# A gated cross-attention and ternary feed-forward kernel: front and second turn as one list, and ternary weights in two passes

## What is computed

```python
x = x + tanh(g_xattn) * xattn(layernorm(x), ctx, mask)    # 16 heads of 32, 77 keys, softmax
x = x + tanh(g_ffn) * ffn(layernorm(x))

def weight_quant(w):                                       # per matrix, 512 x 2048
    scale = 1.0 / clip(mean(abs(w)), 1e-05)
    return clip(round(w * scale), -1.0, 1.0) / scale       # -1, 0 or 1
def act_quant(x):                                          # per token
    scale = 127.0 / clip(max(abs(x)), 1e-05)
    return clip(round(x * scale), -128.0, 127.0) / scale
def ffn(x):                                                # 512 -> 2048 -> 512
    gate = silu(act_quant(x) @ weight_quant(w_gate).T)
    up = act_quant(x) @ weight_quant(w_up).T
    return act_quant(gate * up) @ weight_quant(w_down).T
```

## Time and profile before

| | us |
|---|---|
| median of three runs | 1346.26 |
| lowest, highest | 1342.62, 1346.9 |
| the profiled execution | 1347.23 |
| its span, first to last instruction | 1345.4 |

### The profile page before, as it was taken

One profiled execution on the slowest core, in us unless ns is written; L12 is line 12 of the kernel. 1 busy time (PEld: TensorE's weight loads), 2 busy tenths in 40 slices (PEclk: granted clock), 3 DMA queues, 4 the chain that ended last, 5 costly groups with the idle time before them and its releaser, 6 DMA issues.

```text
span 1345.4 us, 26267 instructions
## 1 busy us (share of the span) xinstructions
PE 1253.8 (93%) x7552; PEld 620.8 (46%) x8126; DVE 1122.8 (83%) x2631; ACT 870.6 (65%) x1350; POOL 737.6 (55%) x1186
## 2 busy tenths in 40 slices
PE   4767699999999999999999999999999999999996
PEld 2223344445454454545454454545445454544542
DVE  6777597897979898897979899797979889796883
ACT  4886756658584766757575665757475665857562
POOL 2104654647475564657466564757566465747662
PEclk9867899999999999999999999999999999999998
DMA  9785348565665658564674756565574847565432
GB/s 327 234 253 114 72 80 172 115 151 115 130 138 111 146 117 169 114 147 113 122 158 89 172 117 150 116 143 124 109 155 109 179 106 152 113 133 98 87 83 67
DMA packets 386793, 181.64 MB, mean 135 GB/s; under 512 B 324323, under 2 KB 357987, under 8 KB 385123
## 3 DMA queue, kind: packets, MB, share of 16 engines
q1 hardware_dynamic: 386736, 181.04, 60.0%
HBM read 61.32 MB, written 35.46 MB: 72 GB/s over the span
## 4 chain that ended last, share of the span: by engine, by line
PE 52%; DVE 18%; DMA 12%; issue 6%; ACT 5%; SPq 4%; POOL 2%; POOLq 0%; ACTq 0%; DVEq 0%
PE bank L1247 16%; PE bank L1259 11%; PE bank L1107 6%; PE bank L1108 6%; PE bank L1109 6%; DMA aT<-ah 6%; PE bank L1186 4%; DVE nmax L987 4%; DVE region L1048 3%; DMA xT<-xh 2%; DVE ah L1011 2%; DVE hmx L1054 2%; POOL work L621 1%; DVE xn L972 1%; ACT work L744 1%
## 5 line engine op out<-in xcount | busy, mean ns | idle before, releaser
L630 POOL TENSOR_TENSOR region<-region,up 128x512 f32<-128x512 f32 x256 | 328.4, 1288 | 290.9 <-DVE region L1048 197.6
L1247 PE MATMUL bank<-tern_gate,region 128*128 128x512 fp8e4 x1024 | 264.6, 381 | 12.3 <-DMA region<-zb 9.3
L1247 PE MATMUL bank<-tern_up,region 128*128 128x512 fp8e4 x1024 | 263.7, 380 | 0.8 <-ACT up L783 0.8
L1259 PE MATMUL bank<-tern_down,region 128*128 128x512 fp8e4 x1024 | 234.5, 382 | 13.7 <-DMA region<-hb 9.6
L1048 DVE SCALAR_TENSOR_TENSOR region<-region,bank 128x512 f32<-128x512 f32 x256 | 170.5, 679 | 79.5 <-ACT region L775 79.2
L775 ACT ACTIVATE region<-bank,fs 128x512 f32<-128x512 f32 x256 | 176.5, 693 | 65.7 <-PE bank L1247 65.6
L621 POOL TENSOR_TENSOR work<-work 124x512 f16<-124x512 f32 x160 | 184.4, 1172 | 26.9 <-ACT work L744 19.9
L1054 DVE TENSOR_REDUCE hmx<-region 128x1 f32<-128x512 f32 x256 | 170.1, 675 | 27.0 <-POOL region L630 26.9
L783 ACT ACTIVATE up<-bank 128x512 f32<-128x512 f32 x256 | 153.9, 602 | 38.0 <-PE bank L1247 37.9
L788 ACT ACTIVATE hb<-region 128x2048 bf16<-128x2048 f32 x64 | 122.8, 1919 | 43.8 <-DVE region L1070 43.8
L1259 PEld LDWEIGHTS bank<-tern_down,region 128*128 128x128 bf16 x1024 | 97.8, 98 | 109.9 <-issue 3.5
(11 more groups left out here) (145 smaller groups left out, 2357.1 us busy)
## 6 DMA issues: line engine op xcount, KB each, us to landing
q_stack<-q_rows SPq DMA_DIRECT2D x96, 256.0 KB, 4.4
xbig<-in_x SPq DMA_DIRECT2D x16, 1024.0 KB, 5.3
q_rows<-q SPq DMA_DIRECT2D x64, 256.0 KB, 3.2
out_y<-o SPq DMA_DIRECT2D x64, 256.0 KB, 3.2
q_stack<-mT SPq DMA_DIRECT2D x32, 256.0 KB, 4.2
region<-in_wgT SPq DMA_DIRECT2D x4, 1024.0 KB, 9.5
region<-in_wuT SPq DMA_DIRECT2D x4, 1024.0 KB, 7.4
region<-in_wdT SPq DMA_DIRECT2D x4, 1024.0 KB, 6.0
```

Source lines behind the costliest of these rows:

```text
L630: nc.gpsimd.tensor_tensor(ht, ht, up[:, n % 2, :], ALU.mult).then_inc(hmul_ready, 1)
L1247: ins = T.matmul(pb[2 * (n % 2) + w][:, :], xqT[:, k, tok], tern[w][:, k * FF + n * GT:k * FF + (n + 1) * GT], start=(k == 0), stop=(k == ...
L1259: ins = T.matmul(pb[2][:, :], hT[:, t % 2, k, :], tern[2][:, k * GT:(k + 1) * GT], start=(k == 0), stop=(k == FK - 1))
```

## The change

1. On every engine the front's list and the second turn's are one list now. The front's parts get three more letters: B is A of group 1, C is N of group 2, K is Q of group 2, and F is the feed-forward part of group 0. `second()` goes. Within the list pieces stand in another order, the front's too.
2. Ternary weights: each quarter is scaled and rounded in one pass on VectorE (`wr`), and ScalarE takes the sign of what is left behind MAGIC, with the constant from a column of `con`. The bounds at -1 and 1, the rounding pass on ScalarE and the semaphores between them go.
3. `mh` has a semaphore of its own, since it stands at another place among VectorE's steps.

GpSimd's list starts as before: `wx`, `wm`, `kx`, the first norm of group 1, `wx`, `vx`, `wm`, `wm`, the subtractions.

```diff
 TENSOR_FIRST = """
-    A:pv00 A:pv01 A:sc13 A:sc14 A:pv02 A:pv03 Q:s30 A:pv10 A:pv11 A:pv12 A:pv13 Q:s31 A:wo00 A:wo10 A:wo20
-    A:wo30 Q:mT00
+    Q:s30 A:pv00 A:sc13 A:pv01 A:sc14 Q:s31 A:pv02 A:pv03 A:pv10 A:pv11 A:pv12 A:pv13 Q:mT00 A:wo00 A:wo10
+    A:wo20 A:wo30 B:sc00 B:sc01 B:sc02 F:gu00 F:gu01 B:sc03 B:sc04 F:gu02 B:sc10 F:gu03 B:sc11 B:pv00 B:pv01
...
 SCALAR_FIRST = """
-    W:wu21 A:ah03 A:ah10 W:wu23 A:ah11 A:ah12 W:wt20 A:ah13 W:wt21 W:wt22 W:wt23 A:zq00 Q:mT00 A:zb00 A:zq10
-    A:zb10 A:zq20 A:zb20 A:zq30 A:zb30
+    W:wt21 A:ah13 W:wt22 Q:mT00 W:wt23 A:zq00 A:zb00 B:sc00 B:sc01 B:sc02 A:zq10 F:up00 F:gu00 F:gu01 A:zb10
+    B:sc03 F:up01 B:sc04 F:gu02 F:gu03 B:sc10 F:up02 B:sc11 F:up03 B:ah00 A:zq20 B:sc12 F:gu10 B:ah01 A:zb20
...
-FRONT = "AMNRQW", {"A": 0, "M": 0, "R": 0, "N": 1, "Q": 1, "W": None}
+FRONT = "AMNRQWBCKF", {"A": 0, "M": 0, "R": 0, "N": 1, "Q": 1, "B": 1, "C": 2, "K": 2, "F": 0, "W": None}
...
-            def weight_round(_, i, j):
-
-                act.wait_ge(wmean_ready, i + 1)
-                nc.scalar.activation(region[:, j * FF:(j + 1) * FF], region[:, j * FF:(j + 1) * FF], ACT.Copy, bias=MAGIC,
-                                     saturate=False, scale=c(R_G + i)).then_inc(wround_ready, 1)
-
             def weight_ternary(_, i, j):
 
-                act.wait_ge(wclip_ready, 4 * i + j + 1)
-                nc.scalar.activation(tern[i][:, j * FF:(j + 1) * FF], region[:, j * FF:(j + 1) * FF], ACT.Copy, bias=-MAGIC,
+                act.wait_ge(wround_ready, 4 * i + j + 1)
+                nc.scalar.activation(tern[i][:, j * FF:(j + 1) * FF], region[:, j * FF:(j + 1) * FF], ACT.Sign, bias=c(MINUS_MAGIC),
                                      saturate=False).then_inc(tern_ready, 1)
...
-            def weight_upper(_, i, j):
+            def weight_round(_, i, j):
 
                 dve.wait_ge(wmean_ready, i + 1)
-                V.tensor_scalar(region[:, j * FF:(j + 1) * FF], region[:, j * FF:(j + 1) * FF], c(R_G + i), 1.0,
-                                ALU.mult, ALU.min).then_inc(wupper_ready, 1)
-
-            def weight_lower(_, i, j):
-
-                if j % 2:
-                    dve.wait_ge(wround_ready, 2 * i + j // 2 + 1)
-                    V.tensor_scalar(region[:, j * FF:(j + 1) * FF], region[:, j * FF:(j + 1) * FF], MAGIC - 1.0, MAGIC + 1.0,
-                                    ALU.max, ALU.min).then_inc(wclip_ready, 1)
-                    return
-                dve.wait_ge(wupper_ready, 2 * i + j // 2 + 1)
-                V.tensor_scalar(region[:, j * FF:(j + 1) * FF], region[:, j * FF:(j + 1) * FF], -1.0, MAGIC,
-                                ALU.max, ALU.add).then_inc(wclip_ready, 1)
+                V.tensor_scalar(region[:, j * FF:(j + 1) * FF], region[:, j * FF:(j + 1) * FF], c(R_G + i), MAGIC,
+                                ALU.mult, ALU.add).then_inc(wround_ready, 1)
...
             turn(TENSOR_FIRST, *FRONT)
-            turn(TENSOR_ORDER, *second())
```

More of the change, by code:

```diff
@@ L531, in _ @@
             pieces["M"], pieces["R"] = pieces["N"], pieces["Q"]
+            pieces["B"], pieces["C"], pieces["K"] = pieces["A"], pieces["N"], pieces["Q"]
             pieces["E"] = pieces["G"] = pieces["H"] = pieces["I"] = pieces["F"]
@@ L539, in _ @@
             turn(SYNC_FIRST, *FRONT)
-            turn(SYNC_ORDER, *second())
             for g in range(2, NG - 1):
@@ L634, in _ @@
             pieces["M"], pieces["R"] = pieces["N"], pieces.get("Q")
+            pieces["B"], pieces["C"], pieces["K"] = pieces["A"], pieces["N"], pieces.get("Q")
             pieces["E"] = pieces["G"] = pieces["H"] = pieces["I"] = pieces["F"]
@@ L643, in _ @@
             turn(POOL_FIRST, *FRONT)
-            turn(POOL_ORDER, *second())
             with pool.Fori(2, NG - 1) as g:
@@ L802, in _ @@
             turn(SCALAR_FIRST, *FRONT)
-            turn(SCALAR_ORDER, *second())
             with act.Fori(2, NG - 1) as g:
@@ L1095, in _ @@
             turn(VECTOR_FIRST, *FRONT)
-            turn(VECTOR_ORDER, *second())
             for g in range(2, NG - 1):
```

87 lines of the change are left out of this document (55 added, 32 removed).

## The result

The changed kernel takes 1348.71 us (median of 20 runs, 1345.49 to 1351.39), the kernel before 1345.00 (median of 20, 1342.62 to 1346.90). The ratio is 1.0028, with a 95% interval of 1.0022 to 1.0035. So the change makes the kernel 3.7 us slower, where 7.5 us of gain were forecast; 1338.8 us and the range up to 1345.0 are both missed. The profiled execution of the changed kernel has a span of 1347.5 us, that of before 1345.4, with nearly equal mean clocks (0.977 and 0.974).

What follows compares the result with a forecast made beforehand. TensorE was taken as the bound from 167.3 us on, so gains lay ahead: cumulatively 0.3, 1.7, 2.6, 5.1, then 7.5 us along the front's chain. 1346.26 - 7.5 = 1338.8 us, range 1331.5 to 1345.

Steps and rivals of the forecast that it cites:

- Part 1: Ternary passes: 12 us off ScalarE, 6.6 off VectorE, little of it on the chain; Sign taken as 1.90 us.
- Part 2: Front up to GpSimd's first subtraction: projection 8 us earlier, sums later; subtraction at 99.4 against 99.74, gain 0.3 us.
- a landing near 76: Group 1's last transpose of x lands near 76, so its query projection starts 8 us earlier than 83.84.
- Rival C: Slower: group 1's projection isn't earlier, its transposes queued behind key transfers and W_up's first quarter; 1350.3 us, chance 0.10.
- 15.7 us from the projection's start to the last sum's end: Group 1's query projection to W_down's last sum on ScalarE: 76 to 91.7, where it was 8.3 us.
- The gap at GpSimd: GpSimd's 6.85 us wait between last reduction and first subtraction taken as fixed after the reduction, whatever the exponentials do.
- Rival A: Front gains too: GpSimd's gap runs beside the exponentials' wait, or projection starts some 4 us earlier; 1334.5 us, chance 0.18.
- Part 3: First subtraction to output projection: subtractions end at 111.3, output projection starts at 119.5; 2.6 us gained in all.
- Part 4: Output projection to first gate matmul: 18.2 us instead of 20.7, gate at 137.7; 5.1 us gained in all.
- Part 5: Second turn's attention: seven score matmuls fill TensorE's gap, first tile's integers done at 161.7 against 170.1; total 7.5 us.
- Rival B: ScalarE's order in the second turn eats the filling, leaving about 3 us of gain; 1343.3 us, chance 0.16.
- From here TensorE's own work sets the end as before, so the gain stays: Behind the first down projection: the whole 7.5 us gain is kept to the kernel's end.

Runs made afterwards that it cites:

- weights_only: Kernel before with only the new ternary passes, all lists in the old order; 1344.69 us, ratio 0.9997.
- scale_behind_q: Changed kernel with one VectorE piece, the scale of W_o, moved behind the low parts of the first two query columns; 1346.05 us, ratio 1.0013.
- one_sum_ahead_x: Changed kernel with W_o's scale later, W_down's last quarter ahead of query rows, two W_down sums earlier, x's load behind the second norm's transpose; 1340.35 us, ratio 0.9964.
- signs_ahead: scale_behind_q with W_up's ternary passes, the W_down loads and three of four W_down sums brought forward; 1351.32 us, ratio 1.0043.
- last_sum_first: signs_ahead with ScalarE's last W_down sum moved directly behind the projection's first output and the transposed maxima; 1349.23 us, ratio 1.0040.
- x_behind_z: Changed kernel with the 1 MB load of group 2's x moved behind the first transpose of z on the queue; 1345.14 us, ratio 0.9999.

## Why the prediction was wrong, point by point

The kernel came out 11.2 us above the forecast (7.5 of gain forecast, 3.7 of loss measured). In the profiles 5.5 us of these are there at the first down projection (172.87, forecast 174.9 - 7.5 = 167.4), and 4.1 us come behind it. The other 1.6 us are the draw: the profiled execution of before, from which the walk was made, was 2.2 us slower than its median, that of the changed kernel 0.6.

- **What bounds the kernel.** Right: from 167 us on TensorE is busy 1011 of 1033 us in the changed kernel as well. But it was 1015 before: nothing could shorten that stretch, and the change made 4.0 us more of idle time in it. All that the experiments moved lies ahead of it.
- **Part 1, ternary weights.** The sizes were right: the Sign passes took 1.99 us (the upper bound, I took 1.90), VectorE's 1.28 (1.31), and there is one table load. That the part gives next to nothing on the chain was wrong in the old order: weights_only's last reduction is 5.1 to 6.4 us earlier. It is no gain of time, though: the ratio is 0.9997 (0.9985 to 1.0010).

```profile
L717 ACT ACTIVATE tern_up<-region,con 128x2048 fp8e4<-128x2048 f32 x4 | 8.0, 1994 | 1.0 <-DVE region L953 1.0
...
L726 ACT ACT_TABLE_LOAD x1 | 1.3, 1283 | 0.7 <-PEq L1328 0.7
```

- **Part 2, the first failed step: "a landing near 76".** It was 79.4. The walk went through the tiles and the transposes and has no term for `wp10`, the 0.15 us operation that waits 6.0 us on VectorE for GpSimd. With it moved the start is 75.5. Rival C (15.7 us fixed behind the projection, each us lost is a us on the end) was the right frame with too low a chance, but the reason that it gave, transposes behind key transfers, isn't what the runs showed.
- **Part 2, the second: "15.7 us from the projection's start to the last sum's end".** 96.5 - 79.4 = 17.1 in the changed kernel and 19.9 in scale_behind_q. I had summed ScalarE's own work and taken the quarters as there. In the changed kernel the last one can be asked for from 82.3 on, when the last ternary pass of W_up is written, goes out behind query rows at 83.23, and takes 11.35 us to land. With it ahead of the rows the distance was 15.9.
- **The gap at GpSimd.** Right: 6.86 us between reduction and subtraction, put to "issue", and the exponentials had been done. Rival A's first half (that the gap runs beside the wait for the exponentials) is out. "Whatever comes" was too simple, see below.
- **Part 3.** 123.86 - 104.14 = 19.7 us from the first subtraction to the output projection, forecast 119.5 - 99.4 = 20.1, before 22.4. 2.6 us were won where 2.3 were forecast, on top of a start that was 4.7 us late.
- **Part 4, the third failed step: "the transpose takes 5.0 us as before".** It took 7.39. 21.4 us from output projection to gate, forecast 18.2. I counted the two DMAs that were moved out of the way and not the megabyte of x that was moved in ahead of the transpose; with it behind, the transpose took 3.17. Most of the other 0.8 us is a later issue, 13.9 us behind the output projection's start where 13.2 were forecast. The lower clock at the gate came nearly as forecast: four gate matmuls in 1.89 us, the next four in 1.61, then 1.03.
- **Part 5.** Better than forecast. Seven score matmuls are done in the gap; the first tile's integers start at 165.57, 20.3 us behind the gate, where it was 25.4 and 22.1 was forecast. The down projection comes 27.6 us behind the gate (32.1 before). Rival B, ScalarE's order eating the filling, didn't come true. But there are other new waits, 1.07 us at 166.23 for VectorE and 1.84 at 195.51 for a transpose, and from 167 to 245 us, where the prediction said to look, TensorE is idle 4.7 us where it was 1.6.

```profile
165.57 1.95 ACT L798 ACTIVATE hb<-region 128x2048 bf16<-128x2048 f32 x1
```

- **The fourth failed step: "From here TensorE's own work sets the end as before, so the gain stays".** 4.1 us are lost behind the first down projection: 2.0 us earlier than before there, 2.1 us later at the end. The cause is open in part, see the next section.

From the changed kernel to one_sum_ahead_x the medians go 1348.7 - 2.7 (scale) - 1.1 (quarter) - 0.5 (sums) - 4.0 (x) = 1340.4. These terms add up by themselves, since each is the step from one median to the next. What tests them is the load of x alone: 3.6 us from the changed kernel, and 1344.4 - 3.6 = 1340.8 was expected before the run, 1340.35 measured. Against before (1345.0 in 20 runs; the forecast started from 1346.26) that is a gain of 4.8 us by the ratio, of the 7.5 forecast.

## What stays open

The down projection of the changed kernel is 2.0 us earlier than before, and its end 2.1 us later. By the last residual of turn 2 some 2.6 us are lost; the largest single wait there is the 1.84 us at 195.51, before group 2's projection. The rest is lost in the loop, in turns in which keys and values of another batch are fetched: 0.9 us in turn 4 and 1.6 in turn 12, but none in turn 8. Measured at the last residual of each turn, the distance to the profile of before grows by 1.1 to 2.8 us from turn 1 to turn 15 in all 15 profiles of kernels with the new ternary passes, weights_only among them, whose loop has the same lists; in a second profile of the kernel before it grows by 0.1. The queue shows one place, in turn 4 (the second profile of before, then weights_only):

```profile
358.07 1.25 SPq L516 DMA_TRANSPOSE region<-zb  x1
360.25 1.29 SPq L453 DMA_DIRECT2D q_stack<-q_rows  x3
```

```profile
355.96 1.25 SPq L515 DMA_TRANSPOSE region<-zb  x1
358.95 1.29 SPq L452 DMA_DIRECT2D q_stack<-q_rows  x3
```

Up to the transpose weights_only leads by 2.1 us, from the query rows on by 1.3. What the query rows wait for there was not found, and no run tested it. Nor does it explain all of weights_only: its profile leads before's by 4.1 us at the gate and 3.0 at the end, or 2.7 and 1.5 against the second profile, while the medians are equal. A part of that lead is the draw of the profiles. The second profile of before:

> The kernel before once more, for one profile. Its profiled execution had been one of the slow ones (1347.2 us against a median near 1345). If the milestones of the front (first subtraction 99.7, output projection 122.1, first gate matmul 142.8) differ here by 2 us or more, differences of that size between two profiles say nothing of a kernel.

The three milestones named there are 98.63, 120.93 and 141.43: 1.1 to 1.4 us earlier, under the 2 us.

## What to carry to other kernels

When work is reordered, walk every engine's list past every moved piece, and ask of each piece that waits what stands behind it: here one 0.15 us operation that waited held VectorE and TensorE for 6 us, and it cost the kernel 2 to 2.7. Then walk the transfer queue with sizes: what counted here for a small transfer on the critical chain is how many megabytes stood just ahead of it when it was asked for (7.39 us with the load of x, 3.17 without; 5.8 behind three quarters of W_down, 3.8 behind one), so a load whose data is needed much later goes behind it. Walk on, too, behind the place where the gain is made: 4.1 us were lost there. And a slow result of a large reordering isn't a verdict on its plan: five pieces moved in the lists turned 3.7 us of loss into 4.8 of gain.

## What was not expected of the hardware

- The gap on GpSimd at a change between plain tensor instructions and partition reductions isn't of one length. Ahead of the second pair of maxima it is 5.8 to 6.1 us in the old order (5.95 in the earlier trace rows) and 8.1 to 9.1 in the new one; behind the last reduction it is 6.9 to 8.5 us, longest in signs_ahead and last_sum_first. The Trainium skill, GPSIMD Engine Reference, section 2.1 (Instruction dispatch), gives about 6 us for the first call to a freshly loaded kernel; the shortest rows agree, the others are up to half as long again. What stretches it is open. Full DMA engines would fit the first place (DMA share from 47 to 57 us 0.60 before, 0.88 in the changed kernel), but not the second: before, 6.85 us at a share of 0.85 (93 to 100 us); signs_ahead, 8.4 us at 0.50 (98 to 106 us).
- A transpose of 128 x 512 by the queue takes from 3.2 to 7.4 us by what stands ahead of it, at the same moment of issue.
- Filling TensorE's gap ahead of the gate with seven score matmuls left the first four gate matmuls at 1.89 us (1.2 GHz) in the changed kernel; in x_behind_z, with 2.0 us of idle time in the gap instead of 5.8, they took 1.04 (2.4 GHz).
